# A second normed buffer, and normed blocks transposed one step earlier, in a two-layer graph attention kernel

## The chip, the cores and the metric

The kernel runs on one core of one Trainium2 chip. The metric is the device time of one launch in microseconds, as the median of several runs. Engines are named as in the profile: PE is TensorE (its weight loads are PEld), DVE is VectorE, ACT is ScalarE, POOL is GpSimd and SP is SyncE, which here only issues DMAs.

## The reference

The input x has 128 graphs of 128 tokens by 256 features, and adj is a 128 x 128 matrix of 0 and 1 for each graph. Two layers follow one another:

```
# layer 0
nx  = layernorm(x) * g1 + b1
q, k, v = nx@wq+bq, nx@wk+bk, nx@wv+bv                      # 8 heads of 32
s   = q k^T / sqrt(32) + where(adj > 0, 0.1*adj*adj, -inf)
x1  = x + softmax(s) v @ wo + bo
out0 = x1 + gelu((layernorm(x1)*g2 + b2) @ w1 + b1) @ w2 + b2   # 256 -> 1024 -> 256
# layer 1
q, k, v = out0@Wq+bq, out0@Wk+bk, out0@Wv+bv
s   = q k^T / sqrt(32), -inf where adj == 0
out = layernorm(out0 + softmax(s) v @ Wo + bo) * gamma + beta
```

Everything is float32.

## The kernel before

The 128 graphs are worked in 32 groups of four ("blocks" b = 0 to 3). A group passes three stages in three successive iterations: A (attention of layer 0), M (the MLP) and C (attention of layer 1). In iteration `it`, stage A works on group it, M on group it-1 and C on group it-2, so there are 34 iterations, of which 30 hold all three stages. Nothing loops at run time: the whole program is written out.

An iteration has eight steps (`STEPS`), and each step has one attention unit (one graph, 8 heads): C blocks 0 to 3 in steps 0 to 3, A blocks 0 to 3 in steps 4 to 7. The class `Shape` (L72 to L134) writes out by hand which operation stands in which step. A unit takes several steps to pass: its scores are made in step k ("unit k"), its probabilities are transposed in step k+1 ("T", two halves g), and they are multiplied with the values ("V", the bank use O) and with the output weight ("W", called the output product) in step k+2. For a C unit the normalisation is applied in the step after W (`late`).

On PE a step runs in this order (L1139 to L1161): `first`, the scores (L1092), V of the unit two back (L1126), `early` and `mid`, T half 0 (L1106), W (L1007), T half 1 (L1106), `fill`. `first`, `early`, `mid` and `fill` are lists of projections:

- Q, K and V of a stage are two operations each. A's stand in steps 0, 1 and 2, C's in steps 5, 6 and 7. In steps with K or Q, one is in `mid` or `early` and the other in `fill`.
- UP 0 to 7 and DOWN 0 are in step 3, DOWN 1 is in step 4.
- XT transposes the four normed blocks of a stage: 8 transposes into two PSUM banks (L1025). XT of A stands `first` in step 0, that of M `first` in step 3, that of C `first` in step 5 (C has no norm of its own ahead of it: its input x_two is what DOWN writes).

Nearly every fp32 operand of a projection is kept as a high and a low part (`HI`, `LO`), and a product is made in three passes. So each PSUM bank is emptied twice: ACT copies the high part out (L584, L587, L598, L608), and then DVE subtracts it from the bank to make the low part (L793, L797, L821, L840). Only when DVE is done does `drained` of the bank rise.

There are four such banks, given out in the order in which `number` (L130) lists the operations; the use n has bank n mod 4. `take` (L993) makes PE wait until the use four before it in this order is drained. `normed` is one buffer, written by every XT and read by the Q, K, V and UP products of the stage. `wait_split` makes each Q, K and UP product wait for both halves of `normed`.

DVE has a long list in each step (L885 to L945): the XT low parts of `first`; the masks of the scores in two halves, 4 heads each (`mask_scores`, L773), with the low part of V's result (`heads_low`, L840) between them; low parts of a Q or K of the `fill` of the step before; the inverse of the first four row sums (`invert`, L783, waits for ACT's exponentials); the late norm (`normalize`, L686); DOWN and UP parts; the copy of the second transposed half (`turned`, L834, waits for PE's T half 1); low parts of early and mid; the second `invert` (waits for ACT's second four exponentials); `add_residual` (L851), followed by the statistics of the block for its norm (`layer_norm_steps`).

M's norm: each A block's `add_residual` is followed by `bn_stats` alone (L857). The rest of the statistics of all four blocks is made at block 3, in step 1 of the next iteration. POOL makes one `rstd` for the four (L480), and in step 2 DVE normalises all four into x_two (L686). Before x_two is overwritten, SP copies it by DMA into res_c, where it is the residual of stage C; POOL adds C's output bias to res_c in step 1 (L501).

ACT: `first` high parts, `heads_high` (L608), exponentials of heads 0 to 3 (L573), high parts of early and mid, `turned` (L603), exponentials of heads 4 to 7, high parts of `fill`. POOL: multiplication of the exponentials with the inverse sums (`make_probs`, L523, two a step), C's gamma and beta (L510, L512), the biases (L501), the `rstd` (L480). All engines run in order and wait on semaphores.

## Time and profile before

The median of three runs is 2387.24 us (2386.19 to 2387.51).

| | us |
|---|---|
| profiled execution | 2387.25 |
| its span, first to last instruction | 2384.8 |
| PE busy | 2208.7 (93%) |
| PEld busy | 1924.1 (81%) |
| DVE busy | 1960.2 (82%) |
| ACT busy | 1700.4 (71%) |
| POOL busy | 1095.8 (46%) |
| mean granted clock of PE | 0.983 |

"Busy" is the time in which at least one instruction of the engine ran. Instructions of one engine overlap by a few tenths of a microsecond, so durations must not be added; where a chain is laid out, the distance from start to start is used. The fortieths of the span look alike from the second to the last but one, at a granted clock of 0.9 or more: the kernel is one iteration repeated.

### The profile page before, as it was taken

What the parts mean: (1) busy time and instruction counts of PE and PEld (TensorE: products, weight loads), DVE (VectorE), ACT (ScalarE), POOL (GpSimd) and SP (SyncE); (2) the same over time, 40 slices, a digit from 0 to 9 for tenths busy, and PEclk for the clock granted to TensorE, in tenths of its full rate; (3) what the DMA queues carried; (4) which work ended last, traced back from release to release, by engine and by line L of the source; (5) the groups of instructions that cost most, each with busy time, mean ns of one, the idle gap of its engine ahead of it and who ended that gap; (6) DMA issues with size and microseconds to landing.
All of it is one profiled execution on the core that took longest, in us unless ns stands there. A gap on an engine that the chain in (4) does not pass through costs nothing.

```text
span 2384.8 us, 62848 instructions
## 1 busy us (share of the span) xinstructions
PE 2208.7 (93%) x22336; PEld 1924.1 (81%) x22336; DVE 1960.2 (82%) x8492; ACT 1700.4 (71%) x5646; POOL 1095.8 (46%) x1159
## 2 busy tenths in 40 slices
PE   4699999999999999999999999999999999999986
PEld 4588888888888888888888888888888888888875
DVE  4588888888888888888888888888888888888775
ACT  2477777777777777777777777777777777777773
POOL 0234544554444455444454454554454455444444
PEclk8799999999999999999999999999999999999988
DMA  3011111111101111101111101111101111110010
GB/s 113 18 33 46 32 33 35 46 42 43 39 28 32 46 46 40 45 22 34 44 46 39 46 24 41 35 46 39 46 31 34 35 46 40 45 38 29 24 33 25
DMA packets 98930, 92.77 MB, mean 39 GB/s; under 512 B 8640, under 2 KB 94272, under 8 KB 98624
## 3 DMA queue, kind: packets, MB, share of 16 engines
q1 hardware_dynamic: 98624, 88.77, 12.1%
q8 instruction: 182, 2.98, 0.5%
q14 instruction: 124, 1.02, 0.1%
HBM read 55.20 MB, written 16.78 MB: 30 GB/s over the span
## 4 chain that ended last, share of the span: by engine, by line
PE 69%; DVE 18%; ACT 8%; issue 4%; POOL 0%; POOLq 0%; DVEq 0%; ACTq 0%
PE p_bank L1007 53%; PE p_heads L1106 7%; DVE normed L793 5%; ACT scores L573 5%; PE p_heads L1092 4%; DVE x_two L686 3%; PE p_bank L1126 3%; DVE scores L773 2%; DVE stats_C L672 1%; PE p_bank L1025 1%; DVE probs_t L834 1%; DVE res_c L851 1%; ACT normed L584 1%; ACT queries_a L587 1%; ACT probs_t L603 1%
## 5 line engine op out<-in xcount | busy, mean ns | idle before, releaser
L523 POOL TENSOR_TENSOR scores<-scores,inverse 128x512 f32<-128x512 f32 x512 | 537.8, 1055 | 715.7 <-DVE inverse L783 715.7
L573 ACT ACTIVATE scores<-scores,negmax 128x128 f32<-128x128 f32 x2048 | 794.9, 393 | 62.6 <-DVE negmax L773 62.2
L573 ACT ACTIVATION_READ_ACCUMULATOR scores<-scores,negmax 128x1 f32 x2048 | 393.1, 192 | 0.0
L1007 PE MATMUL p_bank<-normed,w_up 128*128 128x512 f32 x1536 | 370.1, 397 | 21.7 <-DVE normed L793 21.7
L1007 PE MATMUL p_bank<-w_down,hidden 128*128 128x256 f32 x3072 | 381.4, 284 | 0.0
L1007 PEld LDWEIGHTS p_bank<-w_down,hidden 128*128 128x128 f32 x3072 | 374.2, 190 | 8.6 <-issue 6.0
L1007 PEld LDWEIGHTS p_bank<-normed,w_up 128*128 128x128 f32 x1536 | 285.5, 189 | 89.0 <-issue 29.5
L1106 PE MATMUL p_heads<-ident,scores 128*128 128x128 f32 x2048 | 313.1, 277 | 17.9 <-DVE negmax L773 17.5
L834 DVE COPY probs_t<-p_heads 128x512 f32<-128x512 f32 x256 | 176.0, 687 | 134.1 <-PE p_heads L1106 134.0
L594 ACT ACTIVATE p_bank<-p_bank,ready_cols 128x512 f32<-128x512 f32 x256 | 169.5, 662 | 154.1 <-PE p_bank L1007 148.9
L1106 PEld LDWEIGHTS p_heads<-ident,scores 128*128 128x128 f32 x2048 | 245.0, 142 | 42.0 <-DVE negmax L773 20.3
L1007 PE MATMUL p_bank<-normed,w_k 128*128 128x512 f32 x768 | 211.3, 412 | 53.8 <-DVE normed L793 53.8
L1007 PE MATMUL p_bank<-w_o,heads_t 128*128 128x256 f32 x1536 | 249.4, 299 | 2.9 <-DVE heads_t L840 2.9
L608 ACT ACTIVATE heads_t<-p_bank 128x256 fp32r<-128x256 f32 x256 | 98.5, 385 | 201.4 <-PE p_bank L1126 201.4
L821 DVE TENSOR_TENSOR hidden<-p_bank,hidden 128x512 fp32r<-128x512 f32 x256 | 177.1, 692 | 79.0 <-ACT hidden L598 74.7
L773 DVE CUSTOM_DVE_ANT_0 scores<-p_heads,adj_c 128x128 f32<-128x128 f32 x1024 | 233.2, 287 | 3.1 <-issue 3.1
L773 DVE CUSTOM_DVE_ANT_0 scores<-p_heads,adj_a 128x128 f32<-128x128 f32 x1024 | 235.2, 286 | 0.1
L1007 PEld LDWEIGHTS p_bank<-normed,w_k 128*128 128x128 f32 x768 | 137.4, 192 | 92.8 <-issue 66.9
L1007 PE MATMUL p_bank<-w_v,normed 128*128 128x256 f32 x1536 | 211.9, 288 | 0.0
L603 ACT ACTIVATE probs_t<-p_heads 128x512 f32<-128x512 f32 x256 | 149.7, 585 | 86.7 <-PE p_heads L1106 86.7
L1007 PE MATMUL p_bank<-normed,w_q 128*128 128x512 f32 x768 | 209.6, 409 | 0.0
L1007 PEld LDWEIGHTS p_bank<-w_o,heads_t 128*128 128x128 f32 x1536 | 202.3, 193 | 4.2 <-DVE heads_t L840 4.1
(113 smaller groups left out, 3820.2 us busy)
## 6 DMA issues: line engine op xcount, KB each, us to landing
x_in<-in_x SPq DMA_DIRECT2D x32, 512.0 KB, 3.8
res_a<-in_x SPq DMA_DIRECT2D x32, 512.0 KB, 4.0
res_c<-x_two SPq DMA_DIRECT2D x32, 512.0 KB, 3.3
out<-res_c SPq DMA_DIRECT2D x128, 128.0 KB, 1.7
adj_a<-in_adj SPq DMA_DIRECT2D x32, 256.0 KB, 3.7
adj_c<-in_adj SPq DMA_DIRECT2D x32, 256.0 KB, 2.8
res_c<-in_L_gnn_w SPq DMA_DIRECT2D x1, 512.0 KB, 6.1
values_c<-in_L_gnn_w SPq DMA_DIRECT2D x1, 512.0 KB, 7.0
```

Source lines behind the costliest of these rows:

```text
L523: nc.gpsimd.tensor_tensor(rows_c, rows_c, inverse[:, k % 2, heads].unsqueeze(2).broadcast_to([P, HC, P]), ALU.mult).then_inc(probs_made, 1)
L573: last = nc.scalar.activation(scores[:, k % 2, h], scores[:, k % 2, h], ACT.Exp, scale=-1.0, bias=negmax[:, k % 2, h:h + 1], accum_out=tot ...
L594: nc.scalar.activation(src[:, :], src[:, :], ACT.Gelu, bias=ready_cols[:, 8 + j:9 + j]).then_inc(gelu_made, 1)
L603: nc.scalar.activation(turned_rows(0), turned_columns(0), ACT.Copy).then_inc(turned_out0, 1)
L608: nc.scalar.activation(heads_t[:, HI].rearrange("p c n -> p (c n)"), p_bank[bank][:, 0:KC * P], ACT.Copy).then_inc(high_made, 1)
L773: nc.vector.tensor_tensor_reduce(out=scores[:, k % 2, slot], in0=score_columns(c, j), in1=adj[stage][:, b, :], scale=1.0, scalar=LARGEST, ...
L793: nc.vector.tensor_tensor(lo, src[:, :], hi.bitcast(F32), ALU.subtract).then_inc(drained[bank], 1)
L821: nc.vector.tensor_tensor(hidden[:, j, LO, :], src[:, :], hidden[:, j, HI, :].bitcast(F32), ALU.subtract).then_inc(drained[bank], 1)
L834: nc.vector.tensor_copy(turned_rows(1), turned_columns(1)).then_inc(turned_out1, 1)
L1007: last = nc.tensor.matmul(dst, stationary(i), moving(j), start=(n == 0), stop=(n == total_n - 1))
L1092: last = nc.tensor.matmul(score_columns(c, j), queries[stage][rows_j, i, c, tokens], keys[stage][rows_j, i2, c, tokens], start=(n == 0), s ...
L1106: last = nc.tensor.transpose(turned_columns(g)[:, n // 2, (n % 2) * P:(n % 2 + 1) * P], scores[:, par, HC * g + n, :], ident[:, :])
```

## The change

XT of M, C and A is no longer `first` in a step. A new list `ahead` puts it into the step before: M's into step 2, C's into step 4, and A's of the next group (called N) into step 7. On PE, `ahead` stands between W (the output product) and T half 1; on ACT between `turned` and the second exponentials; on DVE after the low parts of early and mid and before the second `invert` and `add_residual`. In the order of bank uses it stands between W and `fill`. There are two `normed` buffers that alternate. A Q, K or UP product waits for each half of `normed` as it comes to it.

M's norm is made by block: each A block has its own statistics, its own `rstd` on POOL, and is applied in the step after its W (blocks 0 and 1 in step 0, block 2 in step 1, block 3 in step 2). M's XT waits for all four. res_c is no longer filled by DMA: POOL reads x_two, adds the bias and writes res_c, at the start of step 0, ahead of `make_probs`. SP loads the next x after XT N.

```diff
-        self.late, waiting = {}, []
+        self.late, waiting = {}, [-3] if pending else []
...
-        self.first = {0: [("XT", "A")] * a, 3: [("XT", "M")] * m, 5: [("XT", "C")] * m}
+        self.first = {0: [("XT", "A")]} if before is None else {}
+        self.ahead = {2: [("XT", "M")] * m, 4: [("XT", "C")] * m, 7: [("XT", "N")] * (a and following)}
...
-                        + self.mid.get(k, []) + only("W", lag) + self.fill.get(k, []))
+                        + self.mid.get(k, []) + only("W", lag) + self.ahead.get(k, []) + self.fill.get(k, []))
...
+    def normed_room(self, what):
+        return (self.it + (what in "MN")) % 2
...
-        normed = sb("normed", [P, 2, KC, TOK], F32R)
+        normed = [sb(f"normed{i}", [P, 2, KC, TOK], F32R) for i in range(2)]
...
# SP
-                    sp.wait_ge(*drained_use(t, ("XT", "A", 1)))
+                    if s.before is None:
+                        sp.wait_ge(*drained_use(t, ("XT", "A", 1)))
+                    else:
+                        bank, number = t.bank(("XT", "N", 1), earlier=True)
+                        sp.wait_ge(drained[bank], number)
...
-                if s.m:
-                    if s.c:
-                        sp.wait_ge(stored, (t.group_c + 1) * GB * 16)
-                    if not (s.a and s.c):
-                        sp.wait_ge(*drained_use(t, ("DOWN", 1)))
-                    sp.dma_start(res_c[:, :, :], x_two[:, :, :]).then_inc(res_c_loaded, 16)
...
# POOL
-                        if stage == "A" and b == GB - 1:
-                            make_rstd("M", 0, GB, t.group(r) * 3 + 3)
-                        if stage == "C":
-                            make_rstd("C", b, b + 1, (t.group(r) * GB + b) * 3 + 3)
+                        make_rstd("M" if stage == "A" else "C", b, b + 1, (t.group(r) * GB + b) * 3 + 3)
...
+                    if k == 0 and s.c:
+                        wait(pool, stored, t.group_c * GB * 16)
+                        bank, number = t.bank(("DOWN", 1), earlier=True)
+                        add_bias("C", drained[bank], number)
                     for c in range(KC) if k in s.units and k != s.behind else []:
                         make_probs(c)
...
-                    if k == 1 and s.c:
-                        add_bias("C", res_c_loaded, (t.group_c + 1) * 16)
...
# ACT, after turned
+                    for op in s.ahead.get(k, []):
+                        evacuate(t, op)
...
# DVE
-                if stage == "C":
-                    layer_norm_steps("C", x, b, b + 1, (group * GB + b) * 3, True)
-                else:
-                    last = nc.vector.bn_stats(stats["M"][:, b, :], x[:, b, :])
-                    if b == GB - 1:
-                        last.then_inc(ln_steps["M"], 1)
-                        layer_norm_steps("M", x, 0, GB, group * 3, False)
+                layer_norm_steps("M" if stage == "A" else "C", x, b, b + 1, (group * GB + b) * 3)
...
-                elif b == GB - 1:
-                    wait(dve, res_c_loaded, group * 16)
-                    normalize("M", res_a, x_two, 0, GB, group + 1)
+                else:
+                    for b_ in {1: (0, 1), 2: (2,), 3: (3,)}.get(b, ()):
+                        wait(dve, biased["C"], group * 2 - (b_ < 2))
+                        normalize("M", res_a, x_two, b_, b_ + 1, group * GB + b_ + 1)
...
+                    for op in s.ahead.get(k, []):
+                        evacuate(t, op)
                     if k in s.units and k != s.behind:
                         invert(t, k, 1)
...
# PE
-                        wait_split(t, what)
+                        x = normed[t.normed_room(what)]
                         last = three_passes(dst[:, :], [
...
+                            for kc in range(KC)], [split_of(t, what, kc) for kc in range(KC)])
...
                     for op, r in only("W", lag):
                         lagging(t, op, r)
+                    for op in s.ahead.get(k, []):
+                        work(t, op)
                     for _, r in only("T", lag):
                         turn(t, r, 1)
```

## Rows read from the trace of the kernel before

**Rows 1.** The page, busy time of each engine, share of the span and instructions.

```profile
PE 2208.7 (93%) x22336; PEld 1924.1 (81%) x22336; DVE 1960.2 (82%) x8492; ACT 1700.4 (71%) x5646; POOL 1095.8 (46%) x1159
```

**Rows 2.** Waits of PE, whole span: total us, times, longest.

```profile
PE p_bank L1007 <- DVE normed L793: 75.5, 95, 4.5
PE p_bank L1025 <- DVE x_two L686: 34.8, 31, 1.7
```

**Rows 3.** Timeline of PE: start, duration, instructions, [idle before]; steps 5, 0, 1.

```profile
1202.52 1.61 PE L1007 MATMUL p_bank<-normed,w_k 128*128 128x512 f32 x6 [0.99 <-DVE normed L793]
...
1221.81 1.62 PE L1007 MATMUL p_bank<-normed,w_k 128*128 128x512 f32 x6 [0.49 <-DVE normed L793]
...
1226.34 0.89 PE L1092 MATMUL p_heads<-keys_c,queries_c 32*128 32x128 f32 x24
1227.16 0.65 PE L1126 MATMUL p_bank<-probs_t,values_a 128*32 128x128 f32 x16
1227.73 1.65 PE L1007 MATMUL p_bank<-normed,w_q 128*128 128x512 f32 x6
1229.22 0.60 PE L1106 MATMUL p_heads<-ident,scores 128*128 128x128 f32 x4
1229.58 0.96 PE L1007 MATMUL p_bank<-w_o,heads_t 128*128 128x256 f32 x6
1230.37 0.60 PE L1106 MATMUL p_heads<-ident,scores 128*128 128x128 f32 x4
...
1232.30 0.89 PE L1092 MATMUL p_heads<-keys_c,queries_c 32*128 32x128 f32 x24
```

**Rows 4.** Timeline of PE, steps 2 to 5.

```profile
1239.52 1.09 PE L1025 MATMUL p_bank<-ident,x_two 128*128 128x128 f32 x8 [1.10 <-DVE x_two L686]
...
1242.67 3.00 PE L1007 MATMUL p_bank<-normed,w_up 128*128 128x512 f32 x12 [0.66 <-DVE normed L793]
...
1269.58 0.60 PE L1106 MATMUL p_heads<-ident,scores 128*128 128x128 f32 x4
1270.02 1.04 PE L1025 MATMUL p_bank<-ident,x_two 128*128 128x128 f32 x8
...
1273.52 1.61 PE L1007 MATMUL p_bank<-normed,w_k 128*128 128x512 f32 x6 [0.99 <-DVE normed L793]
```

**Rows 5.** Timeline of DVE, steps 5 to 7.

```profile
1207.21 0.41 DVE L851 TENSOR_TENSOR res_c<-p_bank,res_c 128x256 f32<-128x256 f32 x1
...
1208.41 0.29 DVE L773 CUSTOM_DVE_ANT_0 scores<-p_heads,adj_a 128x128 f32<-128x128 f32 x1
...
1209.26 0.42 DVE L840 TENSOR_TENSOR heads_t<-p_bank,heads_t 128x256 fp32r<-128x256 f32 x1
...
1213.33 0.41 DVE L851 TENSOR_TENSOR res_a<-p_bank,res_a 128x256 f32<-128x256 f32 x1
...
1214.12 0.29 DVE L773 CUSTOM_DVE_ANT_0 scores<-p_heads,adj_a 128x128 f32<-128x128 f32 x1
...
1216.16 0.75 DVE L797 SCALAR_TENSOR_TENSOR queries_c<-p_bank,ready_cols,queries_c 128x512 fp32r<-128x512 f32 x1
```

**Rows 6.** Timeline of DVE, later: `turned`, M's norm, low parts.

```profile
1231.01 0.69 DVE L834 COPY probs_t<-p_heads 128x512 f32<-128x512 f32 x1 [0.70 <-PE p_heads L1106]
...
1236.71 2.75 DVE L686 TENSOR_SCALAR x_two<-res_a,moments_M,rstd_M 128x256 f32<-128x256 f32 x4
...
1272.09 1.28 DVE L793 TENSOR_TENSOR normed<-p_bank,normed 128x512 fp32r<-128x512 f32 x2
```

**Rows 7.** Timeline of ACT: first exponential of step 6, and what follows its last.

```profile
1208.95 0.40 ACT L573 ACTIVATE scores<-scores,negmax 128x128 f32<-128x128 f32 x1
...
1213.11 0.69 ACT L587 ACTIVATE queries_c<-p_bank,ready_cols 128x512 fp32r<-128x512 f32 x1
```

**Rows 8.** Timeline of POOL, step 2.

```profile
1235.08 2.54 POOL L501 TENSOR_TENSOR res_c<-res_c,row_bias 128x512 f32<-128x512 f32 x2
1237.58 1.09 POOL L523 TENSOR_TENSOR scores<-scores,inverse 128x512 f32<-128x512 f32 x1
```

More of the change, by code:

```diff
@@ L583, in evacuate @@
                     if kind == "XT":
-                        nc.scalar.activation(normed[:, HI, use[2], :], src[:, :], ACT.Copy).then_inc(high_made, 1)
+                        nc.scalar.activation(normed[t.normed_room(what)][:, HI, use[2], :], src[:, :], ACT.Copy
+                                             ).then_inc(high_made, 1)
                     elif kind in "QK":
@@ L666, in take_wait, with layer_norm_steps @@
                 nc.vector.memset(fence[:, at_col:at_col + 1], 0.0)
-            def layer_norm_steps(n, src, b0, b1, done, measure):
-                if measure:
-                    for b in range(b0, b1):
-                        last = nc.vector.bn_stats(stats[n][:, b, :], src[:, b, :])
-                    last.then_inc(ln_steps[n], 1)
+            def layer_norm_steps(n, src, b0, b1, done):
+                for b in range(b0, b1):
+                    last = nc.vector.bn_stats(stats[n][:, b, :], src[:, b, :])
+                last.then_inc(ln_steps[n], 1)
                 dve.wait_ge(ln_steps[n], done + 1)
@@ L791, in evacuate @@
                         dve.wait_ge(high_made, t.high(use))
-                        hi, lo = normed[:, HI, use[2], :], normed[:, LO, use[2], :]
+                        room = normed[t.normed_room(what)]
+                        hi, lo = room[:, HI, use[2], :], room[:, LO, use[2], :]
                         nc.vector.tensor_tensor(lo, src[:, :], hi.bitcast(F32), ALU.subtract).then_inc(drained[bank], 1)
@@ L997, in take, with split_of @@
                 return bank, p_bank[bank]
+            def split_of(t, what, c):
+                earlier = what == "A" and t.s.before is not None
+                bank, number = t.bank(("XT", "N" if earlier else what, c), earlier=earlier)
+                return drained[bank], number
             def three_passes(dst, products, chunks=None):
@@ L1013, in work @@
                 if kind == "XT":
-                    src = x_in if what == "A" else x_two
-                    if what != "C":
-                        group = t.group_a if what == "A" else t.group_m
-                        pe.wait_ge(ln_applied[what], group + 1)
+                    src = x_in if what in "AN" else x_two
+                    if what == "M":
+                        pe.wait_ge(ln_applied["M"], (t.group_m + 1) * GB)
+                    elif what != "C":
+                        pe.wait_ge(ln_applied["A"], t.group_a + (1 if what == "A" else 2))
                     for i in range(2):
@@ L1037, in work @@
                         w = weight[weights_of[what]["QK".index(kind)]]
-                        wait_split(t, what)
+                        x = normed[t.normed_room(what)]
                         last = three_passes(dst[:, :], [
-                            (lambda i, kc=kc: w[:, i, kc, m * P:(m + 1) * P], lambda j, kc=kc: normed[:, j, kc, :])
-                            for kc in range(KC)])
+                            (lambda i, kc=kc: w[:, i, kc, m * P:(m + 1) * P], lambda j, kc=kc: x[:, j, kc, :])
+                            for kc in range(KC)], [split_of(t, what, kc) for kc in range(KC)])
                     elif kind == "V":
                         w = weight[weights_of[what][2]]
+                        x = normed[t.normed_room(what)]
                         for half_b in range(2):
@@ L1046, in work @@
                             last = three_passes(dst[:, half_b * D:(half_b + 1) * D], [
-                                (lambda i, kc=kc: normed[:, i, kc, b * P:(b + 1) * P], lambda j, kc=kc: w[:, j, kc, :])
+                                (lambda i, kc=kc: x[:, i, kc, b * P:(b + 1) * P], lambda j, kc=kc: w[:, j, kc, :])
                                 for kc in range(KC)])
@@ L1050, in work @@
                         j0 = use[1]
-                        wait_split(t, "M")
+                        x = normed[t.normed_room("M")]
                         last = three_passes(dst[:, :], [
-                            (lambda i, kc=kc: w_up[:, i, kc, j0 * P:(j0 + 1) * P], lambda j, kc=kc: normed[:, j, kc, :])
-                            for kc in range(KC)])
+                            (lambda i, kc=kc: w_up[:, i, kc, j0 * P:(j0 + 1) * P], lambda j, kc=kc: x[:, j, kc, :])
+                            for kc in range(KC)], [split_of(t, "M", kc) for kc in range(KC)])
                     elif kind == "DOWN":
@@ L1067, in hidden_split @@
                 return drained[bank], number
-            def wait_split(t, what):
-                for c in range(KC):
-                    bank, number = t.bank(("XT", what, c))
-                    pe.wait_ge(drained[bank], number)
             def make_scores(t, k):
```

12 lines of the change are left out of this document (6 added, 6 removed).

## The prediction

> **What bounds the kernel.** I read the page's busy times first: PE leads with 93% [rows 1], so the question is what its other 7% are. The waits of PE over the whole span answer it: 75.5 us before products that read `normed`, 95 times, and 34.8 us before M's transposes, 31 times [rows 2]. That is three waits and one in each iteration. The timeline of PE shows all four in one iteration. An iteration lasts 1273.52 - 1202.52 = 71.00 us, and PE stands still for 0.49 us before K of A in step 0, 1.10 us before XT of M, 0.66 us before UP 0, and 0.99 us before K of C in step 5 [rows 3, 4]. Together that is 3.24 us an iteration. All else on PE is back to back, so 110.3 us is the most that the change can win.
>
> Second, how close DVE and ACT stand behind PE. From start to start an undisturbed step of PE costs: scores 0.82, O 0.57, a projection 1.49, T half 0 0.36, W 0.79, and 1.93 for T half 1 and the fill, 5.96 in sum [rows 3]. DVE and ACT have a loop of their own. From the first mask of a step to `add_residual` it is 1213.33 - 1208.41 = 4.92 us (the mask reaches ACT's first exponential after 0.54, ACT needs 4.16 for eight exponentials and two evacuations, then come the second inverse and the residual) [rows 5, 7]. From `add_residual` to the next step's first mask it is 1.20 us behind a C block (full statistics), and 0.79 us behind an A block, which has bn_stats alone [rows 5]. So a C step's loop is 6.12 us, already more than PE's 5.96; an A step's is 5.71. Today the A steps give the lag back.
>
> **The parts, step by step.** I lay one iteration out in the trace's own time, from step 4 on, and compare where UP 0 starts one iteration later: today at 1242.67 + 71.00 = 1313.67 [rows 4].
>
> What I use throughout: from a DVE instruction's end to PE's start 0.15 (1272.09 + 1.28 to 1273.52) [rows 4, 6]; `turned` starts 0.64 after T half 1 starts (1230.37 to 1231.01) [rows 3, 6]; `turned` and each low part occupy DVE for 0.61 from start to start (two low parts take 1.28) [rows 6], the inverse 0.08 (an estimate: 4.92 less 0.54, 4.16 and the hand-over) and `add_residual` 0.40; XT 1.04 [rows 4]. PE needs from DVE in a step, counted from its first mask: four masks for T half 0, done at 0.85 + 0.10; `heads_low` for W, at 0.85 + 0.42 + 0.15 = 1.41 or so; the low part of the previous fill at 1216.16 + 0.75 - 1214.12 = 2.79 [rows 5].
>
> *XT of C, step 4.* It moves to the end of W at 1269.58. Its input was there by 1270.02 at the latest, when today's XT starts with no wait [rows 4], so I take no wait. T half 1 follows at 1270.62, `turned` at 1271.26, low parts at 1271.87 and 1272.48, inverse 1273.08, `add_residual` 1273.16. And here is the new wait: counting banks (DOWN 1, W, XT, XT, O, K), K of C takes the bank of W, which only `add_residual` empties. Before, DVE did that ahead of the low parts; now after them. K starts at 1273.16 + 0.40 + 0.15 = 1273.71, against 1273.52: the 0.99 us is not won, 0.2 is lost. The next masks start 1.20 later, at 1274.36 (today at 1272.09 + 1.21 = 1273.30).
>
> *Steps 5 and 6.* T half 0 waits for masks until 1275.31 (0.11), W for `heads_low` until 1275.77 (0.10), step 6 starts at 1278.49. First masks: 1274.36 + 6.12 = 1280.48 in step 6. W there waits 0.16; step 7 starts at 1284.61, masks 1286.60. In step 6 the residual is an A block's, so the full statistics now cost their 0.41 more, and the lag isn't given back.
>
> *XT of N, step 7.* W runs at 1288.01 to 1288.80. XT takes the bank of the fill of step 6 (Q, O, V, W, XT), drained at 1286.60 + 2.79 + 0.15 = 1289.54: a wait of 0.74 that today's XT hasn't, because there V 1 stands between. T half 1, `turned`, two low parts, the inverse: from XT's start to `add_residual` 1.04 + 0.64 + 0.61 + 1.21 + 0.08 = 3.58, so 1293.12. ACT ends its second exponentials, pushed back by XT's two copies, at about the same time; I add nothing for it. O of step 0 takes W's bank: 1293.12 + 0.55 = 1293.67, where PE alone would be there some 0.5 sooner. K of A starts at 1294.24, today at 1221.81 + 71.00 = 1292.81 [rows 3]. So 0.49 was to be won and 1.43 is lost.
>
> *Step 0.* Masks 1294.32. On POOL a `rstd` (0.5 us, an estimate) and both halves of C's bias, 2.54 us, follow the statistics: 1294.87 to 1297.41, then the first `make_probs`, 1.04, to 1298.45. DVE comes to M's norm of blocks 0 and 1 at 1296.4. In step 2 of today four such norms took 2.75 us: the first two were over only with POOL's bias and its `make_probs` (1237.58 + 1.09 = 1238.67), the last two took 0.4 each [rows 6, 8]. So a norm stands until POOL's instruction is over. By that the two end at 1298.5. `turned` runs behind them to 1299.2, and the scores of step 1 wait for it: start 1299.3 instead of 1298.81. Residual at 1299.91, masks of step 1 at 1301.11. If the norms didn't stand, masks would be at 1294.32 + 6.12 = 1300.44.
>
> The Trainium skill has the same on its page "SBUF — State Buffer", section "Who interferes with whom": DVE in a two-port mode, which a tensor_scalar may use, and a GpSimd instruction exclude each other for a whole instruction. The rows agree. With sharing of bandwidth instead, the sum would be nearer the end without this term.
>
> *Steps 1 and 2.* Step 2 starts at 1305.26, masks 1307.23, W runs 1308.64 to 1309.43. XT of M needs block 3's norm, behind the low part of Q (2.79) with 0.40 of its own: 1307.23 + 2.79 + 0.40 + 0.15 = 1310.57, a wait of 1.14 in place of today's 1.10. It stands one product and one T earlier in PE's order, and its input is no earlier, for the last norm was always one step behind the last block. O of step 3 again takes W's bank: 1310.57 + 3.58 + 0.55 = 1314.70. UP 0 follows at 1315.27. Block 2's norm begins with `make_probs` of the same step and may stand for it, 0 to 0.7, hidden by the wait for T half 1; block 3's likewise, and there it is on the path: I take 0 and keep 0.65 for the range.
>
> *What is hidden.* From UP 0 to the T at 1269.58, 26.9 us of PE work, PE waits for nothing today [rows 4], although DVE has steps 3's and 4's masks and all low parts of UP there. I take the later start of DVE in step 3 (0.7 us behind PE's) as made good there: 0, and the lag is not carried to step 4. The res_c DMA leaves SP's queue, and x is loaded up to a step sooner; no row has PE waiting for a DMA in an iteration: 0. Three more `rstd` on POOL, which is 46% busy [rows 1]: 0. The per-half wait on `normed`: 0, since the bank wait comes later than either half. The longest wait of 4.5 us [rows 2] lies before the first K of the second group, where XT N now goes earlier; between 0 and 4.5, I take 2.3 won.
>
> **Sum.** UP 0 at 1315.27 against 1313.67: 1.60 us longer an iteration. With 31 iterations (the 30 full ones and the two half ones as one) that is 49.6, less 2.3, or 47 us. The profiled execution took 2387.25, the median 2387.24; both give 2435 us. Ends: without the standing norms in step 0 UP 0 comes at 1314.60, 0.93 an iteration, 29 - 2 = 27 us, 2414. With block 3's norm standing as well, 2.25 an iteration, 68 us, 2455.
>
> **Rivals.**
> (a) The lag isn't carried. DVE idles before `turned` (0.70 in the row [rows 6]); if that absorbs the 0.41 of an A block, DVE comes to step 7 as today, XT N finds its bank free (1214.12 + 2.94 = 1217.06 is when W ends today), and nothing stands in step 0. Then step 5 loses 0.2, step 0 is even (O waits 0.5 in place of K's 0.49), and M's transposes wait about 0.75 and O 0.5 in place of 1.10 and 0.66: 0.3 won, some 9 us, and 2 at the start: 2376 us. It decides at a lag of 1.15 us between step 7's start on PE and its first mask. For it: ACT's loop has idle time in A steps. Against it: with full statistics the loop is 6.12 against 5.96, however much DVE idles.
> (b) The change does what it says: bank waits don't bind, and all four waits go. 31 x 3.24 = 100 us: 2287 us. Against it, the bank order.
> (c) The norms never stand: 2414. (d) All stand: 2455.
> (e) The waits only change their name, and gains and losses cancel: 2387.
>
> **Chances.** Forecast 0.42, (c) 0.20, (d) 0.12, (a) 0.11, (b) 0.08, (e) 0.07. Changes within 0.2% (4.8 us) can't be told from none. Slower: 0.42 + 0.20 + 0.12 = 0.74; faster 0.19; same 0.07. Range 2374 to 2458: it takes in (a), (c), (d) and (e), and leaves out (b) and a tail of 0.05. If slower, 2408 to 2458.
>
> **What would show it.** In the profile after: the rows `normed L793` and `x_two L686` lose most of rows 2, except M's transposes, which keep about 1 us each; in their place PE waits at L1126 (O) and at K of C for DVE's res L851, and at XT N for queries_c L797. The period is 72.6 us. M's norms of blocks 0 and 1 take about 1 us each. Wrong if K of C starts without a wait after O, or if the period is below 71.0.

## The result, and the profile after

The changed kernel takes 2418.56 us (median of four runs, 2417.78 to 2420.58) against 2387.38 us of the kernel before in the same comparison. The ratio is 1.0133, 95% interval 1.0115 to 1.0150: slower by 31 us. Forecast: slower, 2435 us, range 2374 to 2458, with 2414 for the case in which the norms in step 0 cost nothing.

The page of the changed kernel, its busy times and then its chain, and last the chain of the kernel before:

```profile
PE 2235.4 (93%) x22336; PEld 1919.0 (79%) x22336; DVE 1971.1 (82%) x8684; ACT 1691.5 (70%) x5646; POOL 1136.1 (47%) x1255
...
PE 43%; ACT 26%; DVE 24%; issue 6%; POOL 0%; POOLq 0%; DVEq 0%; ACTq 0%
...
PE 69%; DVE 18%; ACT 8%; issue 4%; POOL 0%; POOLq 0%; DVEq 0%; ACTq 0%
```

PE is "busy" 27 us longer with the same number of instructions [rows 1]. Nothing was added for it, and the matmuls aren't drawn longer: the mean of one is 397 ns before and 396 after for UP, 299 and 297 for W, 277 and 279 for T. But the profile draws them overlapping (T half 0 is 0.60 us long and W starts 0.36 behind it, in [rows 3]). When a matmul comes a little later, the overlap shrinks, and the union, which is the busy time, grows. So short waits hide in the busy time. The chain that ended last ran through PE for 69% and ACT for 8% of the span before. Now it is 43% and 26%: the chain goes far more through the loop of masks, exponentials and residual.

The waits of PE over the whole span, those that the change made or left (total us, times, longest):

```profile
PE p_heads L1095 <- DVE probs_t L839: 54.5, 67, 2.3
PE p_bank L1033 <- DVE x_two L690: 22.1, 31, 0.7
...
PE p_bank L1129 <- DVE res_a L856: 12.9, 31, 1.2
PE p_bank L1033 <- DVE queries_c L802: 12.3, 30, 0.4
PE p_bank L1129 <- DVE res_c L856: 11.6, 30, 0.4
...
PE p_bank L1014 <- DVE normed L798: 2.9, 3, 1.3
```

The 75.5 us before products that read `normed` [rows 2] are gone but for three waits, as the change meant. M's transposes keep a wait for the last norm (L1033 behind `x_two`), 22.1 of the 34.8 us before, as forecast. Four others are new. Three were in the forecast: O for the bank of W (L1129 behind `res_a` and `res_c`) and XT of N for the bank of the fill (L1033 behind `queries_c`). The largest, scores behind DVE's copy `probs_t`, was forecast for step 1 but not for step 5. The wait that was forecast for K of C behind `res_c` is missing: L1014 waits for it once, 0.2 us.

The timeline of PE through the same iteration as in [rows 3, 4], from the W of step 4 to the next XT of C:

```profile
1209.94 0.95 PE L1014 MATMUL p_bank<-w_o,heads_t 128*128 128x256 f32 x6
1210.74 1.03 PE L1033 MATMUL p_bank<-ident,x_two 128*128 128x128 f32 x8
1211.61 0.60 PE L1109 MATMUL p_heads<-ident,scores 128*128 128x128 f32 x4
1213.08 0.89 PE L1095 MATMUL p_heads<-keys_a,queries_a 32*128 32x128 f32 x24 [0.88 <-DVE probs_t L839]
...
1214.58 1.66 PE L1014 MATMUL p_bank<-normed,w_k 128*128 128x512 f32 x6
...
1219.47 0.89 PE L1095 MATMUL p_heads<-keys_a,queries_a 32*128 32x128 f32 x24
...
1223.63 0.64 PE L1109 MATMUL p_heads<-ident,scores 128*128 128x128 f32 x4
1224.28 1.65 PE L1014 MATMUL p_bank<-normed,w_q 128*128 128x512 f32 x6
1225.86 0.89 PE L1095 MATMUL p_heads<-keys_a,queries_a 32*128 32x128 f32 x24
...
1230.49 1.06 PE L1033 MATMUL p_bank<-ident,x_in 128*128 128x128 f32 x8 [0.44 <-DVE queries_c L802]
...
1234.58 0.65 PE L1129 MATMUL p_bank<-probs_t,values_a 128*32 128x128 f32 x16 [0.39 <-DVE res_a L856]
1235.16 1.66 PE L1014 MATMUL p_bank<-normed,w_k 128*128 128x512 f32 x6
...
1240.49 0.89 PE L1095 MATMUL p_heads<-keys_c,queries_c 32*128 32x128 f32 x24 [0.70 <-DVE probs_t L839]
...
1246.62 0.89 PE L1095 MATMUL p_heads<-keys_c,queries_c 32*128 32x128 f32 x24
...
1251.54 1.09 PE L1033 MATMUL p_bank<-ident,x_two 128*128 128x128 f32 x8 [0.72 <-DVE x_two L690]
...
1255.66 0.64 PE L1129 MATMUL p_bank<-probs_t,values_c 128*32 128x128 f32 x16 [0.39 <-DVE res_c L856]
1256.23 3.03 PE L1014 MATMUL p_bank<-normed,w_up 128*128 128x512 f32 x12
...
1283.18 1.03 PE L1033 MATMUL p_bank<-ident,x_two 128*128 128x128 f32 x8
```

The period is 1283.18 - 1210.74 = 72.44 us, against 71.00.

### The profile page after: what moved, and what is told of

Its sections match the earlier page's. It is cut to its first block, busy times and chain, and to the rows that moved or that the text cites. A ratio compares the mean times of both kernels' runs of the same rounds, so it can differ in the third digit from the quotient of the medians.

```text
span 2416.1 us, 63225 instructions
## 1 busy us (share of the span) xinstructions
PE 2235.4 (93%) x22336; PEld 1919.0 (79%) x22336; DVE 1971.1 (82%) x8684; ACT 1691.5 (70%) x5646; POOL 1136.1 (47%) x1255
## 4 chain that ended last, share of the span: by engine, by line
PE 43%; ACT 26%; DVE 24%; issue 6%; POOL 0%; POOLq 0%; DVEq 0%; ACTq 0%
PE p_bank L1014 33%; ACT scores L575 19%; DVE scores L777 4%; PE p_bank L1033 3%; ACT normed L586 3%; PE p_heads L1109 3%; DVE stats_M L676 2%; DVE res_a L856 2%; ACT probs_t L606 2%; DVE x_two L690 2%; DVE normed L798 2%; PE p_bank L1129 2%; DVE res_c L856 2%; DVE probs_t L839 1%; PE p_heads L1095 1%
## 5 line engine op out<-in xcount | busy, mean ns | idle before, releaser
L1014 PE MATMUL p_bank<-w_down,hidden 128*128 128x256 f32 x3072 | 381.3, 284 | 0.0
L1014 PEld LDWEIGHTS p_bank<-w_down,hidden 128*128 128x128 f32 x3072 | 374.2, 190 | 8.6 <-issue 6.0
L1014 PE MATMUL p_bank<-normed,w_up 128*128 128x512 f32 x1536 | 368.6, 396 | 0.2 <-DVE res_c L856 0.2
L1109 PE MATMUL p_heads<-ident,scores 128*128 128x128 f32 x2048 | 318.3, 279 | 20.2 <-DVE negmax L777 17.7
L1014 PEld LDWEIGHTS p_bank<-normed,w_up 128*128 128x128 f32 x1536 | 283.7, 188 | 65.4 <-issue 5.9
L1109 PEld LDWEIGHTS p_heads<-ident,scores 128*128 128x128 f32 x2048 | 237.7, 142 | 61.8 <-DVE negmax L777 46.4
L1014 PE MATMUL p_bank<-w_o,heads_t 128*128 128x256 f32 x1536 | 248.1, 297 | 3.0 <-DVE heads_t L845 3.0
L1014 PE MATMUL p_bank<-normed,w_k 128*128 128x512 f32 x768 | 212.4, 413 | 3.9 <-DVE normed L798 2.9
L1014 PE MATMUL p_bank<-w_v,normed 128*128 128x256 f32 x1536 | 211.5, 288 | 0.0
L1014 PE MATMUL p_bank<-normed,w_q 128*128 128x512 f32 x768 | 210.8, 410 | 0.1
L1014 PEld LDWEIGHTS p_bank<-w_o,heads_t 128*128 128x128 f32 x1536 | 201.2, 192 | 4.4 <-DVE heads_t L845 4.3
L1014 PEld LDWEIGHTS p_bank<-w_v,normed 128*128 128x128 f32 x1536 | 188.5, 190 | 12.4 <-issue 12.1
```

The costliest lines, as they stand in the source:

```text
L1014: last = nc.tensor.matmul(dst, stationary(i), moving(j), start=(n == 0), stop=(n == total_n - 1))
L1109: last = nc.tensor.transpose(turned_columns(g)[:, n // 2, (n % 2) * P:(n % 2 + 1) * P], scores[:, par, HC * g + n, :], ident[:, :])
```

## Where the 31 us are

ACT loads its table for the gelu once in each iteration that has an MLP, so these loads mark the iterations. Here are the first two and last two, in the kernel before and then in the changed one:

```profile
108.41 1.28 ACT L594 ACT_TABLE_LOAD   x1
...
177.48 1.28 ACT L594 ACT_TABLE_LOAD   x1
...
2236.47 1.28 ACT L594 ACT_TABLE_LOAD   x1
...
2307.22 1.28 ACT L594 ACT_TABLE_LOAD   x1
```

```profile
103.77 1.28 ACT L597 ACT_TABLE_LOAD   x1
...
170.35 1.28 ACT L597 ACT_TABLE_LOAD   x1
...
2270.81 1.28 ACT L597 ACT_TABLE_LOAD   x1
...
2339.54 1.28 ACT L597 ACT_TABLE_LOAD   x1
```

There are 32 of them, so 29 full periods lie between the second and the last but one: (2236.47 - 177.48) / 29 = 71.00 and (2270.81 - 170.35) / 29 = 72.43. That is 41.5 us lost. The edges give back 4.6 before the first load, 2.5 in the first period, 2.0 in the last, and 1.0 behind the last load (2384.8 - 2307.22 = 77.6, 2416.1 - 2339.54 = 76.6). 41.5 - 4.6 - 2.5 - 2.0 - 1.0 = 31.4, the difference of the spans to 0.1.

Part of the 4.5 us won in the first and last period is PE's granted clock and not the order of work: it is 0.98 and 0.91 there in the kernel before, 1.00 and 0.98 in the changed one, and 1.00 in between in both. By the price that e5 shows below (0.88 us for 3.41 us at the lower level), that is some 3 us, an estimate.

## The experiments

Each was compared with the kernel before on its own chip. "Period" is the distance of two XT of M or C in its timeline of PE; except in e5 and e6, the mean over the 29 full periods agrees with it to 0.06 us.

| | median us | ratio to before (95%) | period us |
|---|---|---|---|
| before | 2385.7 to 2387.6 | | 71.00 |
| the change | 2418.56 | 1.0133 (1.0115 to 1.0150) | 72.44 |
| e1 T half 1 first on PE | 2415.64 | 1.0118 (1.0102 to 1.0134) | 72.21 |
| e2 order back on PE, ACT, DVE | 2328.43 | 0.9753 (0.9737 to 0.9768) | 69.49 |
| e3 transposes in old places | 2328.28 | 0.9750 (0.9733 to 0.9768) | 69.24 |
| e4 per-half wait alone | 2352.19 | 0.9853 (0.9838 to 0.9869) | 69.89 |
| e5 order back on ACT, DVE | 2395.61 | 1.0035 (1.0022 to 1.0048) | 71.10 or 71.98 |
| e6 order back on DVE | 2484.72 | 1.0413 (1.0392 to 1.0433) | 73.92, or 74.7 to 75.9 |
| e7 norm by block alone | 2349.18 | 0.9841 (0.9824 to 0.9858) | 69.90 |
| e8 e3 and late norms | 2327.94 | 0.9751 (0.9734 to 0.9768) | 69.30 |
| e9 the change and late norms | 2396.58 | 1.0047 (1.0030 to 1.0064) | 71.73 |
| e10 e3 and late statistics | 2377.17 | 0.9960 (0.9945 to 0.9975) | 70.75 |
| e11 C's transposes back | 2392.80 | 1.0023 (1.0014 to 1.0032) | 71.52 |
| e12 e10 mended | 2300.54 | 0.9639 (0.9626 to 0.9652) | 68.37 |

e5 and e6 carry something that the other runs don't. In 16 of their 29 full periods PE's granted clock falls to its lower level (1.2 GHz of 2.4) for 3.41 us. In e5, K of C in an iteration without such a stretch and in one with it, and the stretch itself (its us, PE busy, PEclk, DMA share, GB/s):

```profile
1200.80 1.63 PE L1014 MATMUL p_bank<-normed,w_k 128*128 128x512 f32 x6 [0.40 <-DVE normed L798]
```

```profile
1271.91 2.40 PE L1014 MATMUL p_bank<-normed,w_k 128*128 128x512 f32 x6 [0.40 <-DVE normed L798]
```

```profile
1272.50:1275.91 3.41, 3.41 (x14) 0.50 0.59 154
```

In the 3.40 us before that fall PE had been busy for 2.13. Such a period takes 0.88 us more in e5; the mean is 71.61 in e5 and 74.53 in e6, so the lower clock costs 0.51 us a period in e5 (15 us in all) and 0.61 in e6 (18 us). The kernel before, the changed kernel and the other experiments have no such stretch between the second and the last but one table load.

**First: is it the moved transposes, their order in the queues, or the norm?** Theory: where the transposes and their two evacuations stand in the queues costs what they win. Rival: the extra DVE work of the norm by block.

e1, on PE only:

```diff
-                    for op in s.ahead.get(k, []):
-                        work(t, op)
                     for _, r in only("T", lag):
                         turn(t, r, 1)
+                    for op in s.ahead.get(k, []):
+                        work(t, op)
```

> The changed kernel with one swap on PE: T half 1 ahead of the moved transposes, the order of ACT and DVE as it is. Theory 1 (order in the queues: where the transposes and their two evacuations stand) splits in two. If what costs is that PE gives T half 1 late, so that DVE's copy of it and the scores that wait for the copy are late, the 0.88 us wait of the scores in step 5 goes, but K of C then waits for the bank of W, which DVE empties only behind both low parts, and it starts within 0.2 us of where it did; steps 0 and 3 start O at the same time, bound by the second exponentials, which ACT still makes behind the transposes' high parts. So under theory 1 the period stays within 0.4 us of 72.4 and the time is 2405 to 2420. The rival (only T half 1 being late matters) expects 0.9 + 0.4 + 0.4 us less a period, 2365 to 2370.

Measured 2415.64, period 72.21: as the theory said. The scores' wait in step 5 went, and K of C took a wait for `res_c L856` (L1014, 31 times, 23.2 us in all) in its place, and O's waits doubled to 0.8. On PE alone the order is nearly free.

e2, the same and on the other two engines:

```diff
# ACT
-                    for op in s.ahead.get(k, []):
-                        evacuate(t, op)
                     if k in s.units and k != s.behind and not long:
                         exps(t, k, 1)
+                    for op in s.ahead.get(k, []):
+                        evacuate(t, op)
# DVE
-                    for op in s.ahead.get(k, []):
-                        evacuate(t, op)
                     if k in s.units and k != s.behind:
                         invert(t, k, 1)
                     for _, r in only("W", lag):
                         add_residual(t, r)
+                    for op in s.ahead.get(k, []):
+                        evacuate(t, op)
```

> The changed kernel with the moved transposes behind T half 1 on PE, their high parts behind the second exponentials on ACT, and their low parts behind add_residual on DVE; still ahead of the fill of the same step, so in the same bank order. Theory 1 (the queue order on ACT and DVE made the new waits): O of steps 0 and 3 no longer waits (0.39 us each), the scores of step 5 don't wait for the copy (0.88), the 0.49 and 0.66 us of the kernel before stay won behind the fill, K of C starts 0.6 us earlier than before by the per-half wait; the wait for the last norm stays at some 0.4 and the lock in step 0 at some 0.7. Period 69.3 to 70.3, time 2335 to 2365. Rival theory 2 (the statistics by block and the standing norms load DVE beyond PE's pace, and the order is unimportant): still 72 or more, 2405 to 2420.

Measured 2328.43, 90 us below the change (and 7 us below the expected range) with every instruction of it kept and three lists reordered. The rival falls.

e3, the change with XT `first` in steps 0, 3 and 5 again (left out here: SP and `split_of` follow the name of XT of A):

```diff
-        self.first = {0: [("XT", "A")]} if before is None else {}
-        self.ahead = {2: [("XT", "M")] * m, 4: [("XT", "C")] * m, 7: [("XT", "N")] * (a and following)}
+        self.first = {0: [("XT", "A")] * a, 3: [("XT", "M")] * m, 5: [("XT", "C")] * m}
+        self.ahead = {}
```

> The change without its moved transposes: XT is first in steps 0, 3 and 5 as before; two normed buffers, per-half waits, M's norm by block and the residual copy by POOL stay. Theory 1: the transposes of M no longer wait for four norms (1.10 us a period won), per-half waits win some 0.5 each in steps 0, 3 and 5, and the statistics and the lock give back 0.5 to 1.0: period 69.0 to 70.0, time 2325 to 2355. Theory 2 (statistics and norms by block are the cost): slower than before, 2400 to 2420.

Measured 2328.28, the same as e2 to 0.2 us. So moving the transposes costs 90 us where the change put them, and wins nothing in the order of e2. The rest of the change is worth 59 us.

**What that rest is.** e4 is the kernel before with the per-half wait:

```diff
-                        wait_split(t, what)
                         last = three_passes(dst[:, :], [
...
-                            for kc in range(KC)])
+                            for kc in range(KC)], [split_of(t, what, kc) for kc in range(KC)])
```

> The kernel before with one edit: each Q, K and UP product waits for the half of normed that it comes to, not for both. A low part takes 0.61 us from start to start, so the first product after each XT should start 0.5 to 0.6 us earlier: 1.5 to 1.7 us a period, 2335 to 2345, if PE is what the next masks wait for least. If instead DVE's loop sets the pace, PE waits for masks or banks a step later and gets back less than half: 2365 to 2387.

Measured 2352.19: 35 us for an edit without any new work. The forecast had put this part at 0 (inside the change the bank wait comes later). The time lies between the two expected ranges. Its period is 1.11 shorter, not the 1.6 expected. The first products of K of A, UP and K of C do start earlier (K of C waits 0.39 us, not 0.99), but of the 0.6 us at K of C only 0.19 is left when XT of A starts (19.67 behind XT of C, against 19.86 before). In steps 6 and 7 T half 0 and the fill come a few hundredths to 0.3 us late; none of it is listed as a wait.

e7 has M's norm by block and the residual copy by POOL without the per-half wait (e3, but each product waits for both halves ahead of its first pass).

> The kernel before with M's norm by block and the residual copy by POOL alone (two normed buffers, no moved transposes, each product waits for both halves as before). If the half wait is worth the 35 us it gave by itself and adds to the norm's part, this is 2328 + 35 = 2363, and the norm by block is a gain of 24 us: 1.10 us a period for M's transposes less the lag of the statistics and the standing norms. If the two depend on each other (the norm pays only where PE's K starts early), it is 2375 to 2390.

Measured 2349.18, a gain of 38 us where 24 was expected. e7 doesn't separate the norm by block from the copy by POOL. 35 and 38 would make 73 together; both together, e3, gave 59. M's transposes no longer wait: the L1025 row of [rows 2], 34.8 us, has no counterpart in the waits of e7 or e3. Its cost, 0.41 us of statistics a block, is there, but it buys off the 2.75 us of four norms in one piece [rows 6].

**Which engine's order.** e5 is e2 without its edit on PE.

> The changed kernel with ACT's high parts of the moved transposes behind the second exponentials and DVE's low parts behind add_residual; PE keeps the change's order, T half 1 behind the transposes. Theory 1a (all three queues must agree: with T half 1 late on PE, DVE's copy of it, and so all behind it, is late whatever DVE does next): the two waits of O (0.39 each) go, the scores' wait of 0.88 in step 5 stays, K of C comes 0.4 later; period 71.3 to 72.2, time 2385 to 2412. Theory 1b (only the orders of ACT and DVE matter, PE's gave 3 us alone): near the kernel with all three moved back, 2328 to 2340.

Measured 2395.61: 23 of the 90 us, or about 38 without the 15 us of the lower clock (an estimate from the periods above). Its undisturbed period, 71.10, lies below the expected 71.3 to 72.2. PE's order alone (e1) gave 3, all three 90, so with or without the clock they don't add up. DVE's copy of T half 1 stands behind PE's transposes (0.88 us in the scores' row of step 5), and all that DVE does after it is late.

e6 is e2 with its edit on DVE alone.

> The changed kernel with DVE's low parts alone behind add_residual; ACT still makes the high parts ahead of its second exponentials. The second inverse waits for these exponentials, so add_residual of steps 7 and 2 comes no earlier (1.4 us behind the copy instead of at once), and the low parts now come 1.2 us later still: K of A in step 0 is late by 0.9. Theory 1a: slower than the changed kernel, 2425 to 2450. Rival (the bank of W, emptied late by DVE's order, is all of it): 2385 to 2400.

Measured 2484.72, 35 us above the range that I gave. Of these 35 the lower clock is 18. The expectation also counted the late low parts in step 0 alone: from XT of N to K of A it is 5.65 us against 4.67 in the change (1263.41 to 1269.06), but from XT of M to UP 0 it is 5.67 against 4.69 as well (1211.09 to 1216.76), and from XT of C to K of C 4.21 against 3.84 (1243.66 to 1247.87). The direction shows the link from ACT to DVE. The chain of waits of e6 through step 2 (start, us, what):

```profile
1211.09 0.89 PE p_bank L1033 x6
...
1212.00 1.09 ACT normed L586 x2
1213.08 1.53 ACT scores L575 x8
...
1214.74 0.42 DVE res_c L856
...
1215.18 0.43 DVE stats_C L676
...
1216.01 0.61 DVE normed L798
```

The high parts hold up the exponentials, these the residual, and with the low parts behind it UP starts only at 1216.76. To reorder DVE's queue and leave the others is the slowest of all the orders tried.

e11 takes back C's transposes alone (`first` in step 5, M's and N's `ahead` as in the change).

> The changed kernel with C's transposes alone back at the start of step 5. Theory 1: ahead of T half 1 they won nothing, since K of C waited for the bank of W, and the scores for the copy; back in place K starts by the half wait 0.5 us earlier than in the changed kernel, and with less lag the small waits of steps 6 and 7 go: 0.5 to 1.2 us a period, 2381 to 2403. Rival (C's place is neutral, the loss comes from N and M): 2412 to 2420.

Measured 2392.80, 26 us below the change. "C's place is neutral" falls. In e11 XT of C starts at 1270.02 and K at 1272.92; with T half 1 ahead of XT again (0.44, as in [rows 4]) K is 3.34 us behind the end of W, against 3.84 in the change: the 0.5 us of the per-half wait. The other 0.4 of a period is won in step 5 too: from K of C to the scores of step 6 it is 4.55 us in e11 (1272.92 to 1277.47) and 4.89 in the change (1214.58 to 1219.47), where the T's and the fill come a little late.

**The term of the standing norms.** e8 (on e3) and e9 (on the change) have the same edit:

```diff
+                    for r in s.late.get(k, []):
+                        apply_norm(t, r)
                     if k in s.units and k != s.behind:
                         invert(t, k, 0)
-                    for r in s.late.get(k, []):
-                        apply_norm(t, r)
...
-                    for b_ in {1: (0, 1), 2: (2,), 3: (3,)}.get(b, ()):
+                    for b_ in {2: (0, 1, 2), 3: (3,)}.get(b, ()):
```

> The change without its moved transposes, and two things more: M's blocks 0 and 1 are normalised in step 1 and not in step 0, and DVE applies norms ahead of its first inverse, so that POOL has not begun make_probs. Lock theory (a norm stands until POOL's instruction is over, 1.05 us each in step 0, 0.37 else): the three norms of step 1 take some 1.1 us in all, the wait of the scores of step 1 (0.3 us) goes and the lag of the steps behind it shrinks: 0.4 to 0.8 us a period, 2303 to 2318. Rival (the time of these norms is their own, or the gap before T half 1's copy covers it): no change, 2326 to 2332, or slower by the later first inverse.

> The changed kernel, its moved transposes kept, with M's blocks 0 and 1 normalised in step 1 and DVE's norms ahead of its first inverse. It prices one term of the prediction: the norms that stand until POOL is done, 2.1 us for two, the scores of step 1 waiting 0.70 us for the copy behind them. The prediction charged 0.67 us a period, 21 us: if the term holds, 2395 to 2402. If what DVE gains there it spends waiting for ACT's exponentials, as when the same edit was made with the transposes in their old places: 2412 to 2422.

All 128 norms of M by the source line (count, then min/median/max ns), in the change and then in e8:

```profile
L690 DVE TENSOR_SCALAR x_two<-res_a,moments_M,rstd_M x128: 382/408/1128, 95.2 to 2334.7; 128x256 f32<-128x256 f32 x128
```

```profile
L686 DVE TENSOR_SCALAR x_two<-res_a,moments_M,rstd_M x128: 401/406/414, 92.1 to 2241.8; 128x256 f32<-128x256 f32 x128
```

No norm of M stands for POOL in e8, and the scores' wait for the copy falls from 15.3 to 5.5 us in all; yet e8 takes 2327.94, what e3 took. In e8's step 0 DVE then waits 0.60 us for ACT's exponentials, so the residual comes only 0.13 earlier behind XT of A than in e3, and the three norms now stand in front of the copy in step 1: the scores of step 2 start 13.58 behind XT of A, against 13.56 in e3. In e9 the same edit is worth 22 us, near the 21 that the prediction charged (0.67 a period). All of it lies where that term was put: from XT of N to XT of M it is 20.36 us in e9 and 21.05 in the change, and the rest of the period is the same to 0.02. The edit also takes the norms' own 0.4 us out of step 0, so this isn't the price of the standing alone. The kernels also differ in what there was to win: one of M's norms takes 723 ns in the mean in the change and 406 in e9, but only 574 in e3, and 406 in e8. One edit has two prices: with the change's order the copy behind the norms is on the path, and with the old order hardly. How the difference divides between the order and the smaller standing isn't separated.

**Is the loop of 6.12 us what remains?** e10 takes the statistics out of it, on e3: DVE makes them behind the masks of the next step, POOL the rstd at the step's start, and the norm is applied behind the copy. Of the edit, DVE's order:

```diff
# DVE
+                    for r in s.late.get(k, []):
+                        statistics(t, r)
                     if k in s.units and k != s.behind:
                         invert(t, k, 0)
-                    for r in s.late.get(k, []):
-                        apply_norm(t, r)
...
+                    for r in s.late.get(k, []):
+                        apply_norm(t, r)
                     if k in s.units and k != s.behind:
                         invert(t, k, 1)
```

> The change without its moved transposes, and with the statistics of a block behind the masks of the next step (DVE adds the residual, makes the next masks, then the statistics; POOL makes the rstd at the step's start; the norm is applied behind the copy of T half 1). Pace theory: from first mask to first mask DVE and ACT take 4.92 + 1.20 = 6.12 us against PE's 5.96, and this loop keeps DVE late at the banks; with the 0.79 us of statistics out of it the loop is 5.3, K of C no longer waits 0.40 and the small waits on banks and masks (0.3 or so, twice) go: 68.1 to 68.6 us a period, 2288 to 2308. Rival (the period of 69.3 is PE's own work and nothing in DVE's order can shorten it): 2322 to 2332.

Measured 2377.17, a miss by 70 us and worse than e3. The timeline of DVE in step 0 and of PE in step 1 of e10 show why:

```profile
1219.25 2.40 DVE L687 TENSOR_SCALAR x_two<-res_a,moments_M,rstd_M 128x256 f32<-128x256 f32 x2 [0.57 <-POOL res_c L496]
```

```profile
1223.07 0.66 PE L1112 MATMUL p_heads<-ident,scores 128*128 128x128 f32 x4 [1.41 <-DVE negmax L774]
```

POOL now began C's bias late, behind the rstd; DVE waited for it, then stood behind it with two norms, and the next masks came 1.41 us late. Steps 5 and 0 had lost their waits as expected. e12 keeps the late statistics and mends this: the bias ahead of the rstd on POOL, M's norms in steps 1 and 2 ahead of the first inverse (`{2: (0, 1), 3: (2, 3)}`), block 3's statistics with its residual as before.

> The statistics behind the next step's masks, once more, without what undid them. In the run before PE stood 1.41 us in step 1 for masks: DVE had waited for POOL's bias of C and then stood behind it with the norms of M's blocks 0 and 1 (2.40 us for two), and 0.68 us before M's transposes for the late norm of block 3. Here POOL adds C's bias ahead of the rstd in step 0; blocks 0 and 1 are normalised in step 1, blocks 2 and 3 in step 2, all ahead of the first inverse; block 3's statistics stay with its residual. Pace theory (DVE's way from mask to mask, 6.12 us against PE's 5.96, is what holds the kernel without moved transposes at 69.3 us): both waits go, 68.0 to 68.6 us a period, 2288 to 2308. Rival (one more wait comes in their place, or the gain of the loop is not PE's): 2322 to 2335, as with the transposes in their old places alone.

Measured 2300.54, ratio 0.9639 (0.9626 to 0.9652): 85 us faster than the kernel before and 118 us faster than the change, the best version. Two rows of the waits of PE in e12:

```profile
PE p_heads L1110 <- DVE probs_t L836: 11.3, 36, 0.9
...
PE p_bank L1029 <- DVE normed L795: 8.9, 7, 4.0
```

The first comes once an iteration, 0.2 us each (six of the 36 are at the edges, where e8 has them too). The second is 7 times in the whole span, where the kernel before had 95: K of C, K of A and UP don't wait. The period is 68.4; that of the kernel before less its four waits [rows 3, 4] is 71.00 - 3.24 = 67.8. e12 differs from e3 in the norms' places too, but e8 moved these on e3 and won 0.3 us, so I put most of the 28 us between e3 and e12 down to the statistics; no run has their place alone.

## Why the prediction was right

The forecast laid out one iteration; here are its times and the measured ones, both counted from the end of the W of step 4 (1269.58 in the forecast, 1210.74 above).

| start on PE | forecast | measured | before |
|---|---|---|---|
| K of C (step 5) | 4.13 | 3.84 | 3.94 |
| step 6 | 8.91 | 8.73 | 8.46 |
| step 7 | 15.03 | 15.12 | 14.42 |
| XT of N | 19.96 | 19.75 | |
| O of step 0 | 24.09 | 23.84 | |
| K of A | 24.66 | 24.42 | 23.23 |
| scores of step 1 | 29.7 | 29.75 | 27.76 |
| scores of step 2 | 35.7 | 35.88 | 33.72 |
| XT of M | 40.99 | 40.80 | |
| O of step 3 | 45.12 | 44.92 | |
| UP 0 | 45.69 | 45.49 | 44.09 |

No start is off by more than 0.3 us, and the excess is 1.40 at UP 0 and 1.44 a period against 1.60. So the main term, evacuations in front of `add_residual` that keep the bank of W full, and a lag that isn't given back, was right. One of the signs that the prediction named for being wrong did come, though: "if K of C starts without a wait after O". It starts 0.67 behind O, where 0.57 is undisturbed, and no wait is listed; the stop stands one unit earlier, at the scores.

- *XT of C, step 4, and the bank of W.* Right in effect, though 0.1 was won and not 0.2 lost. T half 1 starts 0.87 behind XT and not 1.04 (1210.74 to 1211.61). I had missed that the scores of step 5 wait for the copy (`make_scores`, two units back). It costs little of its own here: DVE's copy, low parts and residual run in the same queue, and K waits for the last of them anyway. e1 shows it: the one wait removed, the forecast one appears (0.72 before K of C), and K of C starts 3.66 behind the end of W instead of 3.84.
- *The lag of 6.12 against 5.96.* Right. The chain of waits of the changed kernel (start, us, what) passes through steps 5 and 6 without PE:

```profile
1215.86 1.65 ACT scores L575 x8
1217.51 0.57 ACT keys_c L590
...
1218.57 1.55 ACT scores L575 x8
1220.23 0.42 DVE res_c L856
1220.68 0.43 DVE stats_C L676
...
1221.98 1.65 ACT scores L575 x8
```

  From exponential to exponential that is 1221.98 - 1215.86 = 6.12 us. A further wait from the same lag was missed, the fill of a step for the bank of the fill before (in step 6 T half 1 at 1223.63, Q at 1224.28, 0.65 apart where 0.36 is the plain distance). It is in no list of waits, only in the distances; that the bank is the reason follows from the order of uses and was not tested.
- *XT of N and M, O of steps 0 and 3.* Right, in place and releaser, and the starts agree to 0.25. The waits as listed are shorter than forecast (0.44 for XT of N against 0.74, 0.72 for M against 1.14): part of the time lies in small delays ahead of them.
- *The standing norms.* Right: 2.10 us for two, and 22 us by e9 against the 21 in the sum (with the reserve said there).
- *The edges.* Mis-sized: 10 us won and not 2.3. I took half of one wait at the start; the first and last periods are shorter as well, and some 3 of those 4.5 us are the granted clock, which the forecast didn't look at. With the count of periods (31 taken, 29 like one another) this and the 0.16 a period make up the 16 us between 2435 and 2418.6: 49.6 - 41.5 = 8.1 of it from the periods and 10.1 - 2.3 = 7.8 from the edges.
- *The per-half wait and the norm by block at 0 or as a cost.* True of the sum of this change. By themselves they are the two gains in it, 35 and 38 us. That was not in the prediction, and it needed e4 and e7.

Rival (a), that the lag isn't carried, is refuted by the chain; rival (b) by the rows behind `res_a`, `res_c` and `queries_c`. The 2414 of (c) lies nearer to the result than the 2435 of the forecast, but not for its own reason: the two standing norms took 2.10 us, and e9 shows that they cost about what was charged.

The rows agree with the rule that the prediction cited from the Trainium skill, page "SBUF — State Buffer", section "Who interferes with whom": the norm's longest time, 1128 ns, came with POOL at work (in the changed kernel 62 of M's 128 norms take over 600 ns, each with a POOL instruction running at its start), and in e8, where M's norms run ahead of POOL's instruction, the longest is 414.

## What to carry to other kernels

When an operation moves ahead in one engine's queue, write down what stands behind it on every engine that handles its result, and which bank or copy that work releases. Here 90 us hung on the place of the moved transposes and their evacuations in three queues; moved back on one or two of them alone it gave 3 (PE), 23 (ACT and DVE) and lost 66 (DVE). Where banks are given out in turn, such a dependency arises even between operations with nothing in common. Before moving work to cover a wait, see if the waiting instruction needs all that it waits for: the per-half wait gave 35 us by itself. And where two engines form a loop from step to step, compare its length with the leading engine's step; taking work out of the loop can pay (here the statistics, with the norms' places mended), but only if what it makes late is checked: the same step lost 49 us in e10 and won 28 in e12.

## What was not expected of the hardware

Three readings are worth a note. Waits of 0.1 to 0.3 us don't show as idle time (T half 1 and Q in step 6 of the changed kernel, 0.65 apart for 0.36): PE's busy time rose by 27 us with the same 22336 matmuls. The granted clock fell to 1.2 GHz for 3.41 us in 16 of the 29 full periods of e5 and e6 and in none of the other kernels; before one such fall PE had been busy for 2.13 of 3.40 us, and why just these two kernels is open. And the same edit of the norms was worth 22 us in one kernel (e9) and 0.3 us in another (e8), though it took the standing of M's norms away in both (21 us in e8, 41 in e9).

What stays open: of the 14 us by which e4 and e7 together (73) exceed e3 (59), which of the shared waits carries them; and what the copy by POOL is worth without the norm by block.
